# Attention scores on strips: each score product as four products of 32 output columns

## The reference

```python
scores = jnp.einsum('bhid,bhjd->bhij', q, k) / jnp.sqrt(jnp.float32(D_HEAD))
mask = jnp.tril(jnp.ones((L, L), jnp.float32))[None, None]
scores = scores * mask + (1.0 - mask) * -1000000000.0
probs = jax.nn.softmax(scores, axis=-1)
out = jnp.einsum('bhij,bhjd->bhid', probs, v)
```

## Time and profile before

| | before |
|---|---|
| median of 3 runs | 3622.78 us |
| span of the profiled execution | 3621.2 us |
| PE busy | 3255.9 us (90%), 22839 matmuls |
| PE weight loads | 1559.7 us (43%) |
| DVE busy | 2606.9 us (72%) |
| ACT busy | 1734.9 us (48%) |
| POOL busy | 928.2 us (26%) |
| mean granted PE clock | 0.947 |

### The profile page before, as it was taken

The page is one execution under the profiler, slowest core; times in us unless marked ns, Lnnn a source line. Parts: engine busy times, 40 slices in busy tenths (PEclk is TensorE's granted clock), DMA queues, the critical chain, the costliest instruction groups (busy, mean ns, idle before and its releaser), DMA issues. The chain is left out here.

```text
span 3621.2 us, 79826 instructions
## 1 busy us (share of the span) xinstructions
PE 3255.9 (90%) x22839; PEld 1559.7 (43%) x22839; DVE 2606.9 (72%) x7405; ACT 1734.9 (48%) x3559; POOL 928.2 (26%) x1205
## 2 busy tenths in 40 slices
PE   2888888859999999999999999999998998499999
PEld 1444444413333333333333333333333776265788
DVE  5999999958888888888888888888882555300232
ACT  1444444415767666766766676667666111011000
POOL 4888877721111111111111111111111000201000
PEclk7999989968999999999999999999999999699999
DMA  2566566582434334444344343334442665412000
GB/s 91 156 186 176 171 180 191 167 181 50 95 83 95 80 87 91 91 91 91 91 91 87 85 92 85 82 87 91 91 91 86 232 256 214 150 63 88 3 11 11
DMA packets 173071, 401.91 MB, mean 111 GB/s; under 512 B 34141, under 2 KB 84611, under 8 KB 155927
## 3 DMA queue, kind: packets, MB, share of 16 engines
q1 hardware_dynamic: 152664, 358.73, 37.6%
q10 hardware_dynamic: 18432, 33.56, 2.9%
q0 software_dynamic: 1536, 4.33, 0.4%
HBM read 239.61 MB, written 156.98 MB: 110 GB/s over the span
## 5 line engine op out<-in xcount | busy, mean ns | idle before, releaser
L969 ACT ACTIVATE prob<-ps 128x512 f32<-128x512 f32 (+1 forms) x2560 | 1282.1, 553 | 673.9 <-PE ps L1020 655.0
L892 DVE CUSTOM_DVE_ANT_0 junk<-ps,mask 128x128 bf16<-128x128 f32 (+3 forms) x2048 | 942.5, 486 | 305.5 <-PE ps L1003 285.7
L1003 PE MATMUL ps<-k_rows,q_rows 96*128 96x512 bf16 (+3 forms) x3072 | 937.9, 337 | 78.5 <-DVE mx L892 37.2
L1020 PE MATMUL ps<-q_rows,k_rows 99*128 99x512 bf16 (+3 forms) x3072 | 905.5, 335 | 42.1 <-issue 38.2
L1048 PE MATMUL ps<-prob,v_rows 128*32 128x256 f32 (+1 forms) x11264 | 772.9, 355 | 0.0
L871 POOL TENSOR_SCALAR_AFFINE_SELECT prob<-prob 128x512 f32<-128x512 f32 x512 | 321.8, 640 | 1684.4 <-ACT prob L969 1684.2
L889 DVE TENSOR_REDUCE mx<-ps 128x1 f32<-128x512 f32 x1024 | 687.1, 686 | 41.1 <-PE ps L1003 28.9
L1020 PEld LDWEIGHTS ps<-q_rows,k_rows 99*128 99x128 bf16 x3072 | 275.1, 98 | 600.1 <-ACT prob L969 354.1
L687 PE MATMUL ps<-w_all,x_t 128*128 128x512 f32 (+1 forms) x1024 | 428.6, 543 | 0.0
L1048 PEld LDWEIGHTS ps<-prob,v_rows 128*32 128x32 f32 x11264 | 232.6, 109 | 448.3 <-issue 373.5
L1003 PEld LDWEIGHTS ps<-k_rows,q_rows 96*128 96x128 bf16 x3072 | 298.0, 99 | 267.9 <-DVE mx L892 82.0
(11 more groups left out here) (126 smaller groups left out, 2821.0 us busy)
## 6 DMA issues: line engine op xcount, KB each, us to landing
k_rows<-k_parts SPq DMA_DIRECT2D x384, 128.0 KB, 6.9
v_ones<-v_st SPq DMA_DIRECT2D x64, 512.0 KB, 8.5
v_rows<-v_ones SPq DMA_DIRECT2D x64, 512.0 KB, 8.9
att<-o_sb ACTq DMA_DIRECT2D x128, 256.0 KB, 5.2
att_b<-att SPq DMA_DIRECT2D x16, 2048.0 KB, 9.6
q_parts<-stage SPq DMA_DIRECT2D x192, 128.0 KB, 2.3
k_parts<-stage SPq DMA_DIRECT2D x192, 128.0 KB, 2.4
q_rows<-q_parts SPq DMA_DIRECT2D x64, 384.0 KB, 4.8
```

The lines of the kernel that those rows point to most:

```text
L892: ins = dve.tensor_tensor_reduce(junk[:, at - PS_A, 0:w], src, mask[:, 512 - w:512], 1.0, MASKED, ALU.add, ALU.max, mx[:, g % 2, h, i:i + 1])
L969: nc.scalar.activation(prob[:, (g * NPC + i) % RING, h, 0:w], src, ACT.Exp).then_inc(exp_done, 1)
L1003: pe.matmul(ps[:, chunk_bank(g, c), 0:w], q[0:ROWS, g, h, i * P:(i + 1) * P], k[0:ROWS, g, h, k0:k0 + w], start=True, stop=True).then_inc( ...
L1020: ins = pe.matmul(ps[:, PS_B + bank(g, n), at:at + w], k[0:AUG, g, h, j * P:(j + 1) * P], q[0:AUG, g, h, q0:q0 + w], start=True, stop=True)
```

## The change

Each score product of lines 1003 and 1020, which had a stationary operand of 128 columns, becomes four products of 32 columns, one for each strip of 32 output partitions, with the same moving operand. The weighting has that form already. The outputs, their places and their sums are the same; the semaphore is raised by the last of the four, and the waits stand ahead of the first. With two products to a piece (the form 384 + 128) it becomes eight. The turn of the maxima is left as it is.

```diff
+    STRIP = 2 * DH
...
-                pe.matmul(ps[:, chunk_bank(g, c), 0:w], q[0:ROWS, g, h, i * P:(i + 1) * P],
-                          k[0:ROWS, g, h, k0:k0 + w], start=True, stop=True).then_inc(a_ready, 1)
+                for s in range(0, P, STRIP):
+                    ins = pe.matmul(ps[s:s + STRIP, chunk_bank(g, c), 0:w],
+                                    q[0:ROWS, g, h, i * P + s:i * P + s + STRIP],
+                                    k[0:ROWS, g, h, k0:k0 + w], start=True, stop=True)
+                ins.then_inc(a_ready, 1)
...
                 for j, at, q0, w in PIECES[i][1]:
-                    ins = pe.matmul(ps[:, PS_B + bank(g, n), at:at + w], k[0:AUG, g, h, j * P:(j + 1) * P],
-                                    q[0:AUG, g, h, q0:q0 + w], start=True, stop=True)
+                    for s in range(0, P, STRIP):
+                        ins = pe.matmul(ps[s:s + STRIP, PS_B + bank(g, n), at:at + w],
+                                        k[0:AUG, g, h, j * P + s:j * P + s + STRIP],
+                                        q[0:AUG, g, h, q0:q0 + w], start=True, stop=True)
                 ins.then_inc(b_ready, 1)
```

## The result

The changed kernel takes 3674.53 us (median of 4 runs, 3671.2 to 3678.6) against 3622.33 us for the kernel before beside it: ratio 1.0147, 95% interval 1.0132 to 1.0161. It is slower by 52 us, and the prediction said 3455 us.

What follows compares the result with a forecast made beforehand. PE's chain was taken as the bound; 3.6 us a unit net from removed switches, cut to 2.7 by waits between PE and DVE, over 62 units gives 167 us: 3622.8 to 3455 us, range 3390 to 3590.

Steps and rivals of the forecast that it cites:

- What bounds the kernel: Attention unit of 29.45 us: PE's chain, with 40 array-shape switches around the weighting at 0.095 us, 3.8 us a unit.
- The four-strip round: Score products: four bf16 strips stream side by side at no extra array time; upper bound 15.4 us a unit.
- A: Rival, score products: bf16 strips don't stream at full rate, 512 wide takes 0.43 us; some 4350 us; chance 0.12.
- B: Rival, 128 wide score products: a round takes at least 0.11 us, gain only 1.8 us a unit, 3511 us; chance 0.13.
- D: Rival, weighting switches: the drain belongs to changing between bf16 and f32, so no gap goes; 3620 to 3630; chance 0.05.
- The switch added at the turn: Turn of the maxima, now between strips: costs two switches, 0.19 us a unit, the second beside an existing DVE wait.
- What is late next, and the sum: DVE's 25.80 us matches PE's 25.85; unit 26.75, 2.7 us less, over 62 units 167 us, giving 3455.
- so the fetch stays hidden behind the products: PE's instruction supply: blocks due each 4.3 us against a 2.7 us whole fetch, so added instructions cost no time.
- uncovered: PE's code fetch, if not hidden: 208 more blocks at 1.1 us would be 229 us, all of the gain.
- rival C: Instruction fetch or later last strip at the hand-over eats two of 2.7 us a unit; 3580 us; chance 0.10.
- The slower side: Chance that the changed kernel is slower than before: 0.13, made of A and a bit of D.
- The clock: PE's clock in the loop: below 0.95, because PE now waits for DVE, would also spoil the forecast.

Runs made afterwards that it cites:

- experiment 4: Weighting halves made in one go: kernel before 3643.39 us (1.0056); with strips and PE's loop written out 3513.25; written out without strips 3597.99.
- experiment 6: Changed kernel with later operand loads' bytes left out: 3440.22 us; loads spread in time instead: 3526.19; spread with PE's loop written out: 3414.63; spread without strips: 3621.68.
- experiment 2: Kernel before, without strips, with six unused weight loads of 4 columns added behind each score product: 3803.73 us, ratio 1.0477.
- experiment 1: PE's loop over the 14 middle batches written out: changed kernel 3485.07 us (ratio 0.961); kernel before, without strips, 3595.12 us (0.9919).

## Why the prediction was wrong

**What bounds the kernel.** Right for this change. PE's chain set the pace, and each switch cost 0.09 to 0.10 us: all of it went with the strips, and none with strips of 64. But a switch saved is not always time gained: with long weighting groups half the switches went and the time stayed or rose (experiment 4), so the pace also hangs on when the products reach DVE and ACT.

**The four-strip round.** Right, "I take nothing for the stream": 0.22 between 512 wide products, 0.06 for 128 wide ones. Rivals A, B and D are all refuted by the first six rows of the timeline. The switch added at the turn came as forecast, 0.10 us.

**What is late next, and the sum.** Right where nothing else disturbs. I forecast a unit of 26.75 between 25.85 and 27.3; undisturbed it takes 26.0 in the changed kernel and 26.47 with the bytes left out. There the whole time is 3440 us, where the sum gave 3455: the sum is right for a kernel whose loads are left out, and for no other that was measured.

**The failed step** is "so the fetch stays hidden behind the products". It compared 2.7 us for a fetch with 4.3 us between blocks, an average over the stage. The average itself was on the safe side (some 321 blocks in 1934 us, one in 6.0 us), and it didn't help. But the DMA engines are full for 12 us of each unit, and a block that falls due there comes after more than 400 instructions. I had read the DMA share as 0.43 of a unit and never asked when. The step also took PE's running ahead for a store of code, and did not see that the store empties twice as fast at twice the instructions. The price "uncovered" was in the text, 229 us; I gave it to rival C with three quarters of the gain (2 of 2.7 us a unit) at 0.10, and not as a case that ends slower. What the runs showed in its place is 189 us of stalls for 38, of which 14 for 42 us are left without the loads' bytes. The slower side was spent on A.

**The clock.** I listed its fall as a thing that would spoil it, but as a result of PE waiting for DVE. It came behind the stalls: by the trace's clock records, from the third turn of the maxima to the last, 236 us at 1.2 GHz, for 58.

The account: 62 x (29.45 - 26.47) = 185 us gained; 189 - 38 = 151 us more stalls; 236 - 58 = 178 us more at half rate, which is up to 89 us of work not done. 151 + 89 - 185 = +55 us, and +52 was measured. The first term is seen alone in experiment 6 (-184 us with the bytes left out). The last two are not separated by any run, as each stall brings its clock.

## What to carry to other kernels

An edit that multiplies the instructions of an engine has to be priced against the moments at which its code can't come: look at the code queue's blocks and at the DMA engines together, over one period and not as an average, and count how many instructions the engine gets through in the longest full stretch of DMA. A stall named "issue" in the middle of a product, without a semaphore, was missing code here; that it ends 1.3 to 1.9 us behind a packet of the code queue each time is how to tell. If the edit is otherwise right, the remedy lies in another engine's queue: spreading the loads, worth nothing before, made the strips pay (3526 us), and most with the jumps of PE written out (3415).

## What the runs showed of the hardware

- A strip may run ahead of the others: at 1503.45 one strip of a product starts, and the other three 2.6 us later, after the stall. The first didn't wait for the others to come.
- Six idle weight loads of 4 columns behind a product cost under 0.01 us at 384 and 512 columns and 0.04 to 0.11 us at 128 (experiment 2).
- In the changed kernel's attention 52 of the 65 stalls of 1.5 us and more had a stretch at 1.2 GHz behind them within 5 us; after the other 13, the stalls of 1.7 and 1.6 us that end at 1537.7 and 1545.0 among them, PE stayed at 2.4.
- With PE's loop written out ACT, 49% busy, still stops for its own code at about half of its jumps, 1.5 to 3.0 us each (experiment 1), and DVE in each fourth unit for 2.0 to 2.3 us.
